# Graph attention layer on one core: destination tiles of 128 nodes, T in groups of 512 columns, tensors at multiples of 512 bytes

## The reference, cut to what matters

```python
x1 = layernorm(x)
q, k, v = x1 @ Wq + bq, x1 @ Wk + bk, x1 @ Wv + bv          # (1250, 4, 512) each
alpha = einsum('ehc,ehc->eh', q[dst], k[src]) / sqrt(512)
attn  = softmax of alpha over the edges of one destination   # segment max, sum
agg   = segment_sum(attn[:, :, None] * v[src], dst)          # (1250, 2048)
x_attn = agg + x1 @ Wskip + bskip
h = x_attn @ Wlin + blin + x_attn[:, :512]
x = x + gamma * layernorm(h) + beta
x = x + ffn(layernorm(x))     # three tiny MLPs chosen by flags, one nibble pair is written
```

## Time and profile before

| what | us |
|---|---|
| median of three runs | 1155.57 |
| the profiled execution | 1157.36 |
| its span, first to last instruction | 1155.5 |
| PE busy in the span | 1076.3 |
| DVE, ACT, POOL busy | 569.1, 325.2, 125.3 |

### The profile page before, as it was taken

How to read it: one execution, slowest core, us unless ns; L and a number is a source line. 1 busy time by engine, 2 the same in 40 slices (tenths; PEclk the granted TensorE clock), 3 DMA queues, 4 the chain that set the end, 5 groups by cost and what they waited for, 6 DMA issues and landing times.

```text
span 1155.5 us, 14767 instructions
## 1 busy us (share of the span) xinstructions
PE 1076.3 (93%) x5666; PEld 887.5 (77%) x5666; DVE 569.1 (49%) x1487; ACT 325.2 (28%) x496; POOL 125.3 (11%) x282
## 2 busy tenths in 40 slices
PE   5889999999999999999999999999999999989771
PEld 3666777678888888888888888888888888868550
DVE  4767888553344334234434322433432245676777
ACT  3354443202322223113223212323221132223210
POOL 1201010000000000000000000000000003534464
PEclk9899999999999999999999999999999999999985
DMA  9426364230020020001002000100100010000011
GB/s 294 183 92 217 130 242 168 92 147 1 1 73 1 1 73 1 2 1 73 1 1 73 1 2 1 73 1 1 47 27 1 1 37 9 19 18 23 32 40 33
DMA packets 14206, 64.42 MB, mean 56 GB/s; under 512 B 1939, under 2 KB 2332, under 8 KB 10553
## 3 DMA queue, kind: packets, MB, share of 16 engines
q1 hardware_dynamic: 9529, 46.67, 11.9%
q0 software_dynamic: 4608, 16.78, 3.8%
HBM read 44.11 MB, written 19.34 MB: 55 GB/s over the span
## 4 chain that ended last, share of the span: by engine, by line
PE 69%; DVE 16%; issue 7%; ACT 4%; POOL 2%; DMA 1%; POOLq 0%; DVEq 0%; SPq 0%; ACTq 0%
PE ps_o L1100 7%; PE ps_o L1102 7%; PE ps_o L1101 7%; PE ps_r L1100 7%; PE ps_r L1102 6%; PE ps_r L1101 6%; PE ps_s L1102 5%; PE ps_s L1101 5%; PE ps_s L1100 5%; PE ps_t L1304 3%; DVE opnd_lo L702 2%; PE ps_t L1100 2%; PE ps_t L1102 2%; PE ps_t L1101 2%; ACT prob L667 1%
## 5 line engine op out<-in xcount | busy, mean ns | idle before, releaser
L1100 PE MATMUL ps_s<-xT_hi,tT 128*128 128x512 f32 (+1 forms) x480 | 175.7, 366 | 2.0 <-DVE top L1057 2.0
L1102 PE MATMUL ps_s<-xT_hi,tT 128*128 128x512 f32 (+1 forms) x480 | 170.9, 356 | 0.0
L1101 PE MATMUL ps_s<-xT_lo,tT 128*128 128x512 f32 (+1 forms) x480 | 170.8, 356 | 0.0
L1100 PE MATMUL ps_o<-y,pT 128*128 128x512 f32 x400 | 158.0, 395 | 0.0
L1102 PE MATMUL ps_o<-y,pT 128*128 128x512 f32 x400 | 157.2, 393 | 0.0
L1101 PE MATMUL ps_o<-y,pT 128*128 128x512 f32 x400 | 156.8, 392 | 0.0
L667 ACT ACTIVATE prob<-prob,nbias 125x1250 f32<-125x1250 f32 x40 | 53.7, 1342 | 261.0 <-DVE nbias L1065 261.0
L1057 DVE CUSTOM_DVE_ANT_0 prob<-ps_s,maskb 125x1250 f32<-125x1250 f32 x40 | 58.2, 1456 | 120.5 <-issue 120.5
L622 ACT ACTIVATE pT<-ps_t 128x500 fp32r<-128x500 f32 (+1 forms) x120 | 57.8, 518 | 202.9 <-PE ps_t L1304 202.9
L923 DVE TENSOR_TENSOR pT<-ps_t,pT 128x500 fp32r<-128x500 f32 (+1 forms) x120 | 67.3, 589 | 93.9 <-ACT pT L622 93.9
L1100 PEld LDWEIGHTS ps_s<-xT_hi,tT 128*128 128x128 f32 (+1 forms) x480 | 90.7, 189 | 17.8 <-DVE top L1057 2.5
(11 more groups left out here) (244 smaller groups left out, 1937.0 us busy)
## 6 DMA issues: line engine op xcount, KB each, us to landing
products<-prod_parts POOLq DMA_DIRECT2D x32, 512.0 KB, 3.2
gbuf<-products SPq DMA_DIRECT2D x4, 2048.0 KB, 7.7
mbuf<-products SPq DMA_DIRECT2D x4, 2048.0 KB, 7.9
stage<-in_Wq SPq DMA_DIRECT2D x4, 1024.0 KB, 7.0
stage<-in_Wk SPq DMA_DIRECT2D x4, 1024.0 KB, 5.2
stage<-in_Wskip SPq DMA_DIRECT2D x4, 1024.0 KB, 5.8
stage<-in_Wv SPq DMA_DIRECT2D x3, 1024.0 KB, 4.7
stage<-in_Wlin SPq DMA_DIRECT2D x3, 1024.0 KB, 5.0
```

Of the source, the lines that this page charges most:

```text
L1100: nc.tensor.matmul(out_, a[0], b[0], start=start, stop=False)
L1101: nc.tensor.matmul(out_, a[0], b[1], start=False, stop=False)
L1102: return nc.tensor.matmul(out_, a[1], b[0], start=False, stop=stop)
```

## The change

- `R`, the rows of a destination tile, goes from 125 to 128; ten tiles still, the last with 98 nodes, padded with zeros. Edge tiles stay at 125 (`ER`). The windows of edges of a tile are recomputed: 205 one-hot matmuls instead of 196. x, xres and out move in one DMA of up to 128 rows instead of two (112 and 13).
- T is made in groups of four, four and two tiles: 512, 512 and 226 columns. A job of a 512 group is one part, 12 matmuls of 512 columns, drained by one ACT and one DVE instruction; a job of the 226 group is two parts, 24 matmuls of 226. Steps 1 and 3 make group 1 (two jobs each), steps 5 and 7 group 2 (one job each), steps 10 and 11 the next head's group 0 (two jobs each), and ahead of the loop head 0's group 0 is four jobs instead of two. tT is one tensor of six slots of 128 columns.
- The weights of the 226-column score matmuls are 128 columns wide instead of 125, and the transposes move 128 columns instead of 125.
- pT is one buffer instead of two. POOL's clearing of the pads of xT, tT and pT goes, with PE's wait for it; DVE clears 32 rows of the last x tile at the start instead, and the last x DMA waits for that.
- The first tensor and `arena` start at multiples of 512 bytes.

```diff
-R = 125
-NT = N // R
-ET = E // R
+R = 128
+NT = -(-N // R)
+ER = 125
+ET = E // ER
-GT = 2
-GC = GT * R
+T_GROUPS = [(0, 4), (4, 4), (8, 2)]
+T_SLOT = [2, 3, 4, 5, 0, 1, 2, 3, 4, 5]
+T_SLOTS = 6
+T_COLS = [(0, 512), (512, 512), (1024, N - 1024)]
+SPARE = 2 * ER
...
-    share = ET // NT
-    return range(max(0, share * d - MARGIN), min(ET, share * (d + 1) + MARGIN))
+    share = E * R // N
+    return range(max(0, (share * d - SPARE) // ER), min(ET, -(-(share * (d + 1) + SPARE) // ER)))
...
-        at = [(nc.sbuf_base + 63) // 64 * 64]
+        at = [(nc.sbuf_base + 511) // 512 * 512]
...
+        at[0] = (at[0] + 511) // 512 * 512
         arena = at[0]
...
-        tT = [put(f"tT{i}", [P, 2, KC, GT, P], F32R) for i in range(2)]
-        pT = [put(f"pT{i}", [P, 2, NS, P], F32R) for i in range(2)]
+        tT = put("tT", [P, 2, KC, T_SLOTS, P], F32R)
+        pT = put("pT", [P, 2, NS, P], F32R)
...
+        t_jobs = {1: [(1, 0), (1, 1)], 3: [(1, 2), (1, 3)], 5: [(2, 0)], 7: [(2, 1)]}
+        next_jobs = {NT: [(0, 0), (0, 1)], NT + 1: [(0, 2), (0, 3)]}
...
+        def t_part(g, part):
+            a, w = T_GROUPS[g]
+            return ([part], w) if w == 4 else ([2 * part, 2 * part + 1], w)
...
-            for a, w in ROW_CUTS:
-                sp.dma_start(acc[a:a + w, :, :], x_tiles[a:a + w]).then_inc(x_in, 16)
+            full = R * (NT - 1)
+            sp.dma_start(acc[:, 0:NT - 1, :], x[0:full, :].rearrange("(t p) n -> p t n", p=R)).then_inc(x_in, 16)
+            sp.wait_ge(pads_ready, 1)
+            sp.dma_start(acc[0:LAST_ROWS, NT - 1, :], x[full:N, :]).then_inc(x_in, 16)
...
-            for i in range(2):
-                nc.gpsimd.memset(tT[i][:, :, :, :, R:P].bitcast(F32), 0.0).then_inc(pads_ready, 1)
-                nc.gpsimd.memset(pT[i][:, :, :, R:P].bitcast(F32), 0.0).then_inc(pads_ready, 1)
...
-                for j in range(2):
-                    c = 2 * half + j
-                    ins = nc.scalar.activation(tT[g % 2][:, 0, c, :, 0:R],
...
+                for j, c in enumerate(parts):
+                    ins = nc.scalar.activation(t_slice(0, c, a[0]), t_bank(local, a[0], j), ACT.Identity,
+                                               bias=g0_now[:, c:c + 1])
...
-                for j in range(2):
-                    c = 2 * half + j
+                parts, w = t_part(g, part_)
+                a, cols = T_COLS[g]
+                for j, c in enumerate(parts):
                     for k in range(KC):
-                        ins = mm3(ps_r[:, local % 2, GC * j:GC * j + GC],
+                        ins = mm3(t_bank(local, g, j),
                                   [gbuf[:, s, k, P * c:P * c + P] for s in range(2)],
-                                  [xT[s][:, k, GC * g:GC * g + GC] for s in range(2)], k == 0, k == KC - 1)
+                                  [xT[s][:, k, a:a + cols] for s in range(2)], k == 0, k == KC - 1)
...
-                        m = P if w == BANK else R
-                        ins = mm3(ps_s[0:m, c:c + w], [tT[g % 2][:, s, k, d % GT, 0:m] for s in range(2)],
+                        ins = mm3(ps_s[:, c:c + w], [tT[:, s, k, T_SLOT[d], :] for s in range(2)],
                                   [xT[s][:, k, c:c + w] for s in range(2)], k == 0, k == KC - 1)
...
-            for half in range(2):
-                score_side(0, half - 2, half, 0, first=True)
+            for c in range(KC):
+                score_side(0, c - KC, 0, c, first=c < 2)
...
-            pe.wait_ge(pads_ready, 6)
```

More of the change, by code:

```diff
@@ L69 @@
 NIBBLES = 0x0F0F0F0F
+EDGE_ROWS = [(0, 112), (112, ER - 112)]
 ONE_BITS = 127 * 2.0 ** 23
@@ L322, in graph_layer @@
                     c += 2
-                if k % 2 and k < NT - 1:
-                    fill[last, "t", k] = c
-                    c += 2
+                for job in t_jobs.get(k, []) + ([] if last else next_jobs.get(k, [])):
+                    fill[last, "t", job] = c
+                    highs[last, c] = saved
+                    c += 1
+                    saved += 1
                 if k < 2:
                     fill[last, "y", NT - 2 + k] = c
+                    highs[last, c] = saved
                     c += 1
+                    saved += 1
                 if last and 0 <= k - 4 < NT:
@@ L333, in graph_layer, with t_slice, t_bank @@
         LAST_Y = fill[False, "y", NT - 1]
+        LAST_T = fill[False, "t", t_jobs[7][-1]]
         def side_fills(last, k):
-            if k % 2 and k < NT - 1:
-                return [(fill[last, "t", k] + half, k // 2 + 1, half) for half in range(2)]
-            if not last and k in (NT, NT + 1):
-                return [(8 + k, 0, k - NT)]
-            return []
+            jobs = t_jobs.get(k, []) + ([] if last else next_jobs.get(k, []))
+            return [(fill[last, "t", job], *job) for job in jobs]
+        def t_part(g, part):
+            a, w = T_GROUPS[g]
+            return ([part], w) if w == 4 else ([2 * part, 2 * part + 1], w)
+        def t_slice(s, c, g):
+            a, w = T_GROUPS[g]
+            return tT[:, s, c, T_SLOT[a]:T_SLOT[a] + w, :].rearrange("p t r -> p (t r)")[:, 0:T_COLS[g][1]]
+        def t_bank(local, g, j):
+            return ps_r[:, local % 2, T_GROUPS[g][1] * P * j:T_GROUPS[g][1] * P * j + T_COLS[g][1]]
         def g0_row(h):
@@ L396, in _ @@
                         sp.wait_ge(h_res, t)
-                    for a, w in ROW_CUTS:
-                        sp.dma_start(xres[a:a + w, :], x[R * t + a:R * t + a + w, :]).then_inc(xres_in, 16)
+                    rows = min(R, N - R * t)
+                    sp.dma_start(xres[0:rows, :], x[R * t:R * t + rows, :]).then_inc(xres_in, 16)
                 if t >= 4:
@@ L401, in _ @@
                     sp.wait_ge(o_ready, done + 1)
-                    for a, w in ROW_CUTS:
-                        sp.dma_start(out[R * done + a:R * done + a + w, :],
-                                     acc[a:a + w, done, :]).then_inc(out_done, 16)
-            sp.wait_ge(out_done, 16 * NT * len(ROW_CUTS))
+                    rows = min(R, N - R * done)
+                    sp.dma_start(out[R * done:R * done + rows, :], acc[0:rows, done, :]).then_inc(out_done, 16)
+            sp.wait_ge(out_done, 16 * NT)
         @block.gpsimd
         def _(pool):
-            nc.gpsimd.iota(node_id[0:R, :], [[1, N]], base=0, channel_multiplier=0,
+            nc.gpsimd.iota(node_id[0:ER, :], [[1, XW]], base=0, channel_multiplier=0,
                            allow_small_or_imprecise_dtypes=True).then_inc(ids_ready, 1)
@@ L900, in rotating_lo @@
             def rotating_lo(h, local, kind, a, last=False):
-                highs = local if local < LAST_Y or not last or kind == "y" else NT + 2 * (a[0] - 1) + a[1]
-                dve.wait_ge(rot_hi, rot(h, highs) + 1)
+                dve.wait_ge(rot_hi, rot(h, highs.get((last, local), local)) + 1)
                 if kind == "y":
@@ L1036, in tail @@
                     moments(k - 3, acc[0:R, k - 3, :], z_var)
-            for half in range(2):
-                rotating_lo(0, half - 2, "t", (0, half, 0))
+            for c in range(KC):
+                rotating_lo(0, c - KC, "t", (0, c, 0))
             def head(h, last):
@@ L1166, in cd_by_rows @@
                 pe.wait_ge(packed_ready, NT)
-                for c, w in COLS:
+                for c, w in COLS[0:2] + [(COLS[2][0], XW - COLS[2][0])]:
                     for k in range(KC):
@@ L1258, in _, with score_side @@
                 skip_tile(t)
-            def score_side(h, local, half, g, first=False):
+            def score_side(h, local, g, part_, first=False):
                 r = rot(h, local)
@@ L1316, in outputs @@
                         pe.wait_ge(pt_free, 3 * n + 4)
-                    ins = mm3(ps_o[:, :], [pT[d % 2][:, s, t, :] for s in range(2)],
+                    ins = mm3(ps_o[:, :], [pT[:, s, t, :] for s in range(2)],
                               [y[:, s, t, :] for s in range(2)], t == 0, t == NS - 1)
@@ L1337, in head @@
                     if not last and d == NT + 1:
-                        score_side(h, 19, 1, 0)
+                        for local, g, part_ in side_fills(last, d):
+                            score_side(h, local, g, part_)
                     if 0 <= d - 2 < NT:
```

103 lines of the change are left out of this document (47 added, 56 removed).

## The result

The changed kernel takes 1148.87 us (median of 5 runs, 1148.49 to 1149.91), the kernel before, on the same chip in the same comparison, 1155.57 (1154.95 to 1157.66): a ratio of 0.9942 with a 95% interval of 0.9928 to 0.9956, so 6.7 us faster. The forecast was 1149.4. The profiled execution of after took 1148.49 with a span of 1146.7, 8.8 us less than the profiled one of before; 2 of these 8.8 are the difference of the two executions from their medians.

A forecast was written before the change was run, and what follows sets the result against it. PE's pace was taken to bound all but the last head from step 4. Three heads -8.3, head 3 -1.4 and -1.6, group 0 +5.3, skip tiles -0.7, one-hots +0.8, x +0.1, output DMA -0.4: 1155.6 - 6.2 = 1149.4 us, range 1144 to 1153.

The forecast's parts named there:

- What bounds the kernel: PE's own pace sets the head loop; the loop through DVE, POOL and ACT sets head 3 from step 4.
- Places: With xT and arena at multiples of 512, values and scores take 0.227 us a matmul; with outputs, 2.4 us less per head.
- The sign within T: 250-column matmuls take 0.1169 us in step 3 and 0.1138 in step 7, where only the operand's start differs.
- T: Larger groups in the head loop: 0.9 us less per head, with the stall in step 1 staying.
- 128 columns: Wider weights and transposes in each head: narrow scores +0.24 us, transposes +0.3 us.
- Last head: Head 3: -1.4 us to step 3; from step 4, shorter drains in steps 5 and 7, -0.8 each, -1.6.
- Ahead of the loop: Before the head loop: group 0 as four jobs +5.3 us, skip tiles -0.7, one-hot matmuls +0.8, transposes of x +0.1.
- the one-hots: In the product stage, nine matmuls more of 209 columns: +0.8 us, up to 3 if each waited for DVE.
- Rival A: The new starts of xT and arena do nothing to the pace of values and scores: 1160 us, chance 0.15.
- C: Equal starts collide: values, scores, T and outputs slow from 0.227 to 0.235 us, 1170 us, chance 0.04.
- B: Multiples of 512 bring matmuls to the bare 0.213 us: 1106 us, chance 0.06; in part, 1120 to 1143, 0.07.
- D: T jobs wait for drains in steps 1 and 10, 0.5 us more each: +3, 1152 to 1153 us, chance 0.08.

The follow-up runs named there:

- the window experiment: The kernel before with the ninth window of edge tiles four tiles longer (126 to 149 instead of 126 to 145), the last unchanged: 1153.96 us in one run.

## Why the prediction was right, and where not

That the median fell by 6.7 where 6.2 was forecast is in part luck. Between the two profiled executions the span fell by 8.8: the head loop gained 1.3 less than forecast and the part ahead of it did 3.9 better, and the medians stand 2.2 closer together than the two traces do.

*What bounds the kernel* held. The head loop gained what PE's matmuls gained; the last head behind its fifth maximum gained only where a drain became shorter, and leaving out 80 matmuls there changed nothing.

*Places* was the right mechanism with a term mis-sized. From start to next start, a turn's 120 values take 27.37 us instead of 28.10, a gain of 0.73 as said (0.76). The 240 scores of 512 columns take 56.40 instead of 57.29: 0.89, not 1.42. The pace was read in steps 0 and 1, where the earlier trace rows are, and taken for all ten steps, and behind transposes only about half the gain is left. Outputs 0.30 (0.24). The sign within T that I leaned on, 0.1169 against 0.1138, was a weaker one than I made it: with the distance at 0 in the kernel before, group 4 did slow to 0.117 (48 in 5.60 us), but group 0 took 5.67 us for 5.72, next to nothing. It pointed to places and not to how they count. Skip tiles gained their 0.77, but perhaps not for the start alone, the reason that I gave: tile 8 of before had the distance 0 and was slow, and the weights also went from 125 to 128 columns.

*T*: 0.87 a head against 0.9 (28.31 us for 29.17), with the narrow ones at 0.112 as taken; the stall in step 1 stayed. *128 columns*: narrow scores +0.28 (0.24), transposes +0.16 (0.3). Together 2.35, and the turn shrank by 2.3 where the forecast said 2.8; the scores are the difference. Over three turns that is 1.3 us less gain.

*Last head*: -0.7 to the fifth maximum and -1.8 behind it, forecast -0.5 and -1.6. Order of time on DVE in after:

```profile
999.60 1.46 DVE L1067 CUSTOM_DVE_ANT_0 prob<-ps_s,maskb 128x1250 f32<-128x1250 f32 x1
...
1004.82 0.81 DVE L922 SCALAR_TENSOR_TENSOR tT<-ps_r,g,tT 128x226 fp32r<-128x226 f32 x2 [3.31 <-ACT tT L624]
1005.55 1.45 DVE L1082 CUSTOM_DVE_ANT_0 prob<-prob,count 128x1250 f32<-128x1250 f32 x1
...
1022.10 1.46 DVE L1067 CUSTOM_DVE_ANT_0 prob<-ps_s,maskb 128x1250 f32<-128x1250 f32 x1
...
1025.41 1.46 DVE L1082 CUSTOM_DVE_ANT_0 prob<-prob,count 128x1250 f32<-128x1250 f32 x1 [1.41 <-ACT prob L678]
...
1041.98 1.46 DVE L1067 CUSTOM_DVE_ANT_0 prob<-ps_s,maskb 128x1250 f32<-128x1250 f32 x1
```

A step with a T job takes 22.50 us, one without 19.88: the two numbers of the forecast (22.5 and 19.8), against 23.31 and 19.83 in the earlier trace rows. With T, maximum to product is 5.95 instead of 3.31.

*Ahead of the loop*: group 0 cost 5.24 us more (forecast 5.3), skip tiles 0.77 less (0.7). The step that failed is the one-hots: +0.8 forecast, up to 3, and the stage of the products ended 2.6 us earlier. I counted nine matmuls more and thought of waits only as something that grows; the windows also moved the work of DVE between stages, and PE's time at the one-hots shrank by 3.2 us from the fourth to the eleventh product. The products' own matmuls took 0.4 more, so the stretch gained 2.7. Of this the window experiment shows 0.9; the rest recurs in every kernel with the new windows, but what in them does it stays open.

*The rest*: the tail gained 0.1, forecast 0.4. Of the 3.9 that the part ahead of the loop did better than forecast, 3.5 lie at the one-hots (2.7 less for 0.8 more) and recur; so the 2.2 us between traces and medians are not there. The profiled execution of before was 1.8 above its median, and no trace of a faster one of that kernel shows where the others save; the last section has the stretch that points to it.

Two slips in the rivals' sums change no forecast: the bare pace would also reach all 576 matmuls of the products, not 432 (46 us in place of 44), and A and C together are 0.19, where the last line has 0.16 for slower. Rival A was refuted by undoing the places, B (0.213) and C by the paces at distance 0 (0.2267, and outputs at 68.3 us a turn for 68.6), D by T jobs that wait no more than before.

## What to carry over

Read a matmul's pace from start to start and by pairs of operands; where the same shape has two paces at one clock, print where the two operands start and look at their distance modulo 64 before anything else is rearranged; then measure, since with 125 columns of weights or 226 columns of data the distance bought nothing here. Take a pace from every surrounding in which the matmul stands, not from the cleanest one. When tiles or windows are resized, count for each stage what the other engine has to deliver new, not only what PE consumes; and a longer first group is paid in full ahead of the loop, so make the first one short and put the second where the drains cost nothing.
